# Mamba in a macaron block: the residual is added by TensorE and copied by ScalarE, the normalisation's shift is made by GpSimd

## What is computed

```
x = x + 0.5 * moe(layernorm(x))
x = x + mamba(layernorm(x), weights 1) + mamba(flip(layernorm(x)), weights 2)
x = x + 0.5 * moe(layernorm(x))

mamba: xi, z = split(x @ in_w.T)
       xc    = silu(causal_conv4(xi) + conv_b)              # 256 inner channels
       dt, B, C = split(xc @ xp_w.T)                        # 8, 16, 16
       delta = softplus(dt @ dtp_w.T + dtp_b)
       h_t   = h_{t-1} * exp(delta_t * A) + delta_t * xc_t * B_t      # 16 states
       y     = (sum over states of h_t * C_t + xc * D) * silu(z)
       return y @ out_w.T
```

## Time and profile before

| | |
|---|---|
| Time, median of 3 runs | 2934.28 us (2933.41 to 2934.28) |
| Profiled execution | 2933.32 us, of which its span is 2931.5 us |
| Busy over the span | PE 84%, DVE 85%, POOL 78%, ACT 54%, PEld 52% |
| Mamba's units in the span | about 559 to 2392 us |
| Mean granted PE clock | 0.95 of full speed |

### The profile page before, as it was taken

The page is one execution under the profiler, slowest core; times in us unless marked ns, Lnnn a source line. Parts: engine busy times, 40 slices in busy tenths (PEclk is TensorE's granted clock), DMA queues, the critical chain, the costliest instruction groups (busy, mean ns, idle before and its releaser), DMA issues.

```text
span 2931.5 us, 37910 instructions
## 1 busy us (share of the span) xinstructions
PE 2458.6 (84%) x10844; PEld 1533.2 (52%) x10844; DVE 2495.6 (85%) x3793; ACT 1575.0 (54%) x2744; POOL 2297.3 (78%) x1360
## 2 busy tenths in 40 slices
PE   4799999688888888888888888888888875899993
PEld 2799998233343443344344334433433335899993
DVE  6766666499999999999999999999999988666666
ACT  3355555566556565655656565565656541555551
POOL 1577777489889988889899898889888853777772
PEclk8899999899999999999999999999999988999997
DMA  6011112223333333233233333222322340111116
GB/s 222 14 49 49 49 49 47 72 96 96 105 97 94 96 104 99 94 99 106 87 102 105 92 95 106 97 94 95 102 93 90 99 149 1 45 48 50 49 49 190
DMA packets 159360, 254.71 MB, mean 87 GB/s; under 512 B 22114, under 2 KB 64002, under 8 KB 158594
## 3 DMA queue, kind: packets, MB, share of 16 engines
q1 hardware_dynamic: 140338, 209.21, 22.8%
q0 software_dynamic: 18464, 37.79, 4.8%
q10 hardware_dynamic: 432, 6.29, 0.5%
HBM read 219.65 MB, written 33.55 MB: 86 GB/s over the span
## 4 chain that ended last, share of the span: by engine, by line
DVE 29%; issue 21%; PE 15%; POOL 11%; ACT 5%; DMA 1%; POOLq 0%; DVEq 0%; SPq 0%
DVE buf L830 11%; PE bank L1333 7%; DVE buf L821 6%; DVE bank L806 6%; POOL buf L396 5%; ACT over L1072 3%; POOL buf L454 3%; POOL token_outputs L406 2%; PE bank L1329 2%; PE bank L1275 2%; PE bank L1283 2%; ACT L1043 1%; PE bank L1189 1%; DVE buf L794 1%; DVE X L717 1%
## 5 line engine op out<-in xcount | busy, mean ns | idle before, releaser
L454 POOL TENSOR_TENSOR buf<-buf 128x1024 f32<-128x1024 f32 x512 | 1202.6, 2360 | 197.8 <-DVE buf L830 164.2
L1333 PE MATMUL bank<-buf,id_sb 128*128 128x512 f32 x2048 | 1017.0, 626 | 133.3 <-POOL buf L454 130.5
L830 DVE TENSOR_TENSOR_SCAN buf<-over,bank 128x512 f32<-128x512 f32 x768 | 892.3, 1203 | 1.0
L1072 ACT ACTIVATE over<-wgu,negA 128x510 f32<-128x510 f32 x768 | 505.8, 712 | 555.0 <-DVE buf L830 483.0
L1333 PEld LDWEIGHTS bank<-buf,id_sb 128*128 128x128 f32 x2048 | 395.1, 198 | 568.1 <-issue 350.9
L806 DVE TENSOR_TENSOR bank<-wgu,bank 128x512 f32<-128x512 f32 x768 | 487.2, 681 | 2.5 <-POOL wgu L486 2.5
L1208 PE MATMUL bank<-parts 128*128 128x256 f32 x3456 | 486.4, 291 | 3.2 <-DVE buf L680 1.6
L1208 PEld LDWEIGHTS bank<-parts 128*128 128x128 f32 x3456 | 434.2, 192 | 7.1 <-issue 4.0
L406 POOL DMA_INDIRECT token_outputs<-buf,slot_out x288 | 293.1, 1018 | 110.7 <-issue 85.3
L396 POOL DMA_INDIRECT buf<-token_rows,slot_token x288 | 301.1, 1046 | 96.7 <-issue 90.1
L821 DVE TENSOR_TENSOR_SCAN buf<-bank,buf 128x256 f32<-128x256 f32 x512 | 309.0, 665 | 44.4 <-ACT bank L1081 43.9
(11 more groups left out here) (155 smaller groups left out, 2308.8 us busy)
## 6 DMA issues: line engine op xcount, KB each, us to landing
buf<-state_rows SPq DMA_DIRECT2D x640, 256.0 KB, 3.2
token_rows<-buf SPq DMA_DIRECT2D x32, 256.0 KB, 2.3
y_pair<-token_outputs SPq DMA_DIRECT2D x16, 512.0 KB, 5.1
buf<-token_outputs SPq DMA_DIRECT2D x16, 512.0 KB, 5.0
buf<-token_rows,slot_token POOLq DMA_INDIRECT x288, 2.6
token_outputs<-buf,slot_out POOLq DMA_INDIRECT x288, 2.3
out<-X SPq DMA_DIRECT2D x16, 256.0 KB, 3.9
wgu<-wgT ACTq DMA_DIRECT2D x1, 2048.0 KB, 8.4
```

Source lines behind the costliest of these rows:

```text
L454: pool.tensor_tensor(hC[:, b, :].rearrange("p (c w) -> p c w", c=C), hs[:, b, :].rearrange("p (c w) -> p c w", c=C), Cs[:, b, :].unsqueeze ...
L830: V.tensor_tensor_scan(hs[:, b, w], dA[:, b, c, :, :].rearrange("p s t -> p (s t)"), bank[c], 0.0, ALU.mult, ALU.add).then_inc(s[f"scan_do ...
L1072: ins = A.activation(dA[:, n % R, c, :, 1:], delta[r][:, c * W:(c + 1) * W].rearrange("p (s t) -> p s t", s=S)[:, :, 1:], ACT.Exp, scale=n ...
L1333: ins = M.matmul(bank[4 + c], id_sb[:, :], hC[:, n % R, c * W:(c + 1) * W], start=False, stop=(n == NS - 1), skip_group_check=True)
```

## The change

Three things are changed.

- `project_out` on PE gets, for each of the four tiles, one more matmul that adds X to bank 7 through the identity. It has one more wait, for the residual of the unit before (it reads the X which that one wrote).
- `post_residual` on DVE is removed. ACT copies bank 7 to X instead (`residual`) at the same state, 8, and for the last unit ahead of the second mixture-of-experts part.
- `mean_shift` on DVE is removed. POOL's `rstd` makes -mean ahead of var + eps, and -mean times rstd behind the power, both 128x4. `normalise` waits for that.

```diff
-DVE_AT = {"gate": 2, "stats": 5, "lo": 8, "res": 8, "shift": 9, "size": 12}
+DVE_AT = {"gate": 2, "stats": 5, "lo": 8, "size": 12}
-ACT_AT = {"silus": 4, "hi": 7, "parts": 10, "ln": 11, "xn": 12, "scale": 13, "xnT": 15}
+ACT_AT = {"silus": 4, "hi": 7, "res": 8, "parts": 10, "ln": 11, "xn": 12, "scale": 13, "xnT": 15}
...
             def rstd(p):
                 pool.wait_ge(s["dve_norm"], done(DVE_NORM, "aggr", p))
                 pool.sem_inc(s["rstd_turn"], 1)
+                pool.tensor_scalar(ve[:, G:2 * G], MV[:, :, 0], -1.0, None, ALU.mult)
                 pool.tensor_scalar(ve[:, 0:G], MV[:, :, 1], EPS, None, ALU.add).then_inc(s["vareps_pre"], 1)
                 pool.wait_ge(s["vareps_pre"], p + 1)
                 pool.tensor_tensor(rs[:, 0:G], ve[:, 0:G], half[:, 0:G], ALU.pow).then_inc(s["rstd_pre"], 1)
+                pool.wait_ge(s["rstd_pre"], p + 1)
+                pool.tensor_tensor(shift[:, :], ve[:, G:2 * G], rs[:, 0:G], ALU.mult).then_inc(s["shift_pre"], 1)
...
-            def mean_shift(p):
-                dve.wait_ge(s["rstd_pre"], p + 1)
-                dve.wait_ge(s["dve_norm"], done(DVE_NORM, "aggr", p))
-                V.scalar_tensor_tensor(out=shift[:, :], in0=MV[:, :, 0], scalar=-1.0, in1=rs[:, 0:G],
-                                       op0=ALU.mult, op1=ALU.mult).then_inc(s["dve_norm"], 1)
...
-            def post_residual(u, p, r):
-                dve.wait_ge(s["pe_post"], u + 1)
-                xp4 = X[:, bass.ds(p * G, G), :]
-                V.tensor_tensor(xp4, xp4, bank[7].rearrange("p (t d) -> p t d", t=G),
-                                ALU.add).then_inc(s["res_done"], 1)
...
-                act.wait_ge(s["dve_norm"], done(DVE_NORM, "shift", p))
+                act.wait_ge(s["shift_pre"], p + 1)
...
+            def residual(u, p):
+                act.wait_ge(s["pe_post"], u + 1)
+                A.activation(X[:, p * G:(p + 1) * G, :], bank[7].rearrange("p (t d) -> p t d", t=G),
+                             ACT.Copy).then_inc(s["res_done"], 1)
...
+                        if n == ACT_AT["res"] and not (first and r == 0):
+                            residual(p * 2 + r - 1, p - 1 if r == 0 else p)
...
             pair(NP - 1, False, True)
+            residual(2 * NP - 1, NP - 1)
             act.wait_ge(s["res_done"], 2 * NP)
...
             def project_out(u, r, after):
                 pe.wait_ge(s["gated"], u + 1)
+                wait(pe, s["res_done"], u)
                 after()
                 for t in range(G):
                     for c in range(C):
-                        ins = M.matmul(bank[7][:, t * D:(t + 1) * D], gat[:, c * W + t * P:c * W + (t + 1) * P],
-                                       out_sb[:, r, c, :], start=(c == 0), stop=(c == C - 1))
+                        M.matmul(bank[7][:, t * D:(t + 1) * D], gat[:, c * W + t * P:c * W + (t + 1) * P],
+                                 out_sb[:, r, c, :], start=(c == 0), stop=False)
+                    ins = M.matmul(bank[7][:, t * D:(t + 1) * D], id_sb[:, :], X[:, (u // 2) * G + t, :],
+                                   start=False, stop=True)
                 ins.then_inc(s["pe_post"], 1)
```

More of the change, by code:

```diff
@@ L38 @@
     "conv0_", "conv1_", "z0_", "z1_", "xdbl", "dt0_", "dt1_")]
-DVE_NORM = ["stats", "aggr", "shift"]
+DVE_NORM = ["stats", "aggr"]
 ACT_NORM = ["xn", "xnT", "xnTrev"]
-DVE_AT = {"gate": 2, "stats": 5, "lo": 8, "res": 8, "shift": 9, "size": 12}
+DVE_AT = {"gate": 2, "stats": 5, "lo": 8, "size": 12}
 POOL_AT = {"first": 0, "second": 1, "rstd": 7, "du": 13}
-ACT_AT = {"silus": 4, "hi": 7, "parts": 10, "ln": 11, "xn": 12, "scale": 13, "xnT": 15}
+ACT_AT = {"silus": 4, "hi": 7, "res": 8, "parts": 10, "ln": 11, "xn": 12, "scale": 13, "xnT": 15}
 PE_AT = {"conv": 0, "z": 5, "xdbl": 6, "out": 7, "dt": 9, "xt": 13}
@@ L260, in macaron_kernel @@
             experts_done expA_done pair_added dtp_zeroed diag_ready taps_spread taps_ready skip_ready gated du_done dve_pre
-            act_pre pe_pre vareps_pre rstd_pre res_done pe_post negA_done bcB_ready bc_copied bc_stored C_in0 C_in1 C_in2 C_in3 B_in0 B_in1 dA_ready
+            act_pre pe_pre vareps_pre rstd_pre shift_pre res_done pe_post negA_done bcB_ready bc_copied bc_stored C_in0 C_in1 C_in2 C_in3 B_in0 B_in1 dA_ready
             dP_ready0 dP_ready1 mul_done pool_mul_done scan_done0 scan_done1 hC_ready y_done""".split()
@@ L569, in moe @@
                     if m == 1 and j == 0:
-                        post_residual(2 * NP - 1, NP - 1, 1)
                         dve.wait_ge(s["res_done"], 2 * NP)
@@ L846, in pair @@
                             product(p, r, n + 1)
-                        if not (first and r == 0):
-                            if n == DVE_AT["res"]:
-                                post_residual(u - 1, p - 1 if r == 0 else p, 1 - r)
                         if not prep:
@@ L858, in pair @@
                                 layernorm(p + 1)
-                            if n == DVE_AT["shift"]:
-                                mean_shift(p + 1)
             layernorm(0)
-            mean_shift(0)
             split_lo(0, 0)
```

## The result

| | before | after |
|---|---|---|
| Time, median | 2934.28 us (4 runs, 2933.41 to 2936.96) | 2893.24 us (4 runs, 2890.67 to 2893.94) |
| Ratio to before | | 0.9855, 95% interval 0.9843 to 0.9866 |
| Profiled execution (its span) | 2933.32 us (2931.5) | 2893.94 us (2892.1) |

The change makes the kernel 41.0 us faster, 39.4 us by the profiled executions; 44.1 was predicted, and 2890 us for the time. In the kernel after, the lines are L784 for the gate, L820 for the scan, L811 for the scan of POOL's four states, L796 for the product, L772 for `split_lo`, L457 for `times_C`, L444 for POOL's product, L1070 for the decay into a bank, L1061 for the other decays and L1051 for the residual's copy.

The account below looks back on a forecast made before the run. DVE, 97% busy in the Mamba part, was taken to bound it from state 8's scan to the next gate, PE and ACT before that. 22.7 + 21.8 - 0.4 = 44.1 us off 2933.32 gave 2889.2, median 2890, range 2885 to 2896.

Parts of the forecast that it names:

- The loop of two parts: Mamba unit: PE and ACT set the time from gate to state 8's scan, DVE from there to the next gate.
- Residual: DVE at state 8: removing the addition saves 0.71 us in each of 31 units, 22.0 us.
- Shift: DVE at state 9: removal saves 21.8 us over 15, nearly all of it waiting for POOL's instruction to end.
- Shift on POOL: POOL at state 7 of 15 units: the new work takes 0.6 us (0.3 to 2.0) and costs nothing in the units.
- The far end of 2.0 us: Highest price of POOL's new work at state 7; state 11's product would still come 0.2 us before its scan.
- the cover at state 11: POOL's product for state 11, with 0.6 us of new work ahead, still has 1.6 us to spare before DVE's scan.
- X through PE, residual on ACT: State 7 matmuls, 1.0 us, and ACT's copy, 0.58 us, cost nothing; without cover 31 and 18.6 us.
- First pair and last residual: First pair's shift on POOL costs 0.4 us; the 32nd residual, in the second mixture-of-experts part, saves 0.7 us.
- The clock rival: PE's chain behind the gate at 1.2 GHz: 12.7 us more a unit, 2954 us with five; chance 0.04.

Follow-up runs that it names:

- e8: Kernel after plus an unused 128x512 DVE reduction at state 6 of every unit: 2896.19 us, ratio to before 0.9862.
- e9: Kernel after plus an unused 128x512 DVE reduction at state 10 of every unit: 2914.91 us, ratio to before 0.9924.
- e2: Kernel before with only the shift moved from DVE to POOL: 2912.81 us against 2937.24 before, ratio 0.9919.
- e6: Kernel after plus an unused 128x4 DVE operation with two SBUF inputs at state 9 of first directions: 2902.12 us, ratio to before 0.9881.
- e7: Kernel after plus an unused 128x4 DVE maximum with one SBUF input at state 9 of first directions: 2902.22 us, ratio to before 0.9883.
- e1: Kernel after with the shift back on DVE at state 9, so only the residual's half: 3079.31 us on a slower chip, ratio to before 0.9957.
- e11: Kernel after plus two unused 128x4 powers on POOL ahead of the shift's multiplication: 2915.62 us, ratio to before 0.9922.
- e3: Kernel before with PE's four extra matmuls, DVE copying bank 7 instead of adding it: 3093.55 us against 3093.14 before, ratio 1.000.
- e4: Kernel after with a second ACT copy of bank 7, ahead of the residual's: ratio to before 0.9875.
- e5: Kernel after with PE's whole output projection made twice into the same bank: ratio to before 0.9849.

## Why the prediction was right, and where a size was off

*The loop of two parts.* Right. The idle time ahead of the scan of state 8 stayed at 0.71 and 1.99 us, both removed steps lay behind it, and e8 and e9 show the same work free ahead of it and full price behind it.

*Residual.* This is the mis-sized term. The start-to-start 0.71 us of the removed instruction was taken as what its removal gives. It isn't, because the instruction behind it then meets another neighbour: `split_lo` can't overlap the product as the residual could. Measured is 0.60 (1.89 to 1.29): 31 x 0.60 = 18.6 instead of 22.0 us, 3.4 less (18.3, 3.7 less, by the gates). It is the largest mechanism in the 3.2 us between 2890 and 2893.24; the books below have the rest.

*Shift.* Right. A pair of units went from 113.93 to 111.18, so 2.75 us less, of which 1.18 are two residuals (0.59 each by the gates) and 1.57 the shift. Fourteen shifts lay between the first gate and the last: 22.0 us, as e2 has it by itself; 21.8 was predicted for fifteen. The fifteenth is in the first unit, where it met the end of POOL's instruction (0.20 us, which the mean of 1.53 holds), and gave nothing: the way to the first gate was 64.52 and is 64.54 us from the first product. e6 and e7 confirm the reason. What the prediction left out is that this wait also takes back gains ahead of it: by e1 the residual alone gives 10.1 us between the gates, 12 but for its late units, and not the 22.0 of its term. Because both parts were made together, the sum of the two terms holds; for the residual alone the same working would have promised nearly double.

*Shift on POOL.* Right: 0.23 and 0.20 us, 0.55 with their issue (0.6 predicted), and no DVE idle time for POOL. The far end of 2.0 us was costed at nothing, and no run tests it. e11's wait bears out the cover at state 11 (2.2 us), but its 2.7 us cost 20 in all, twice what first directions explain, by late units that the working does not have.

*X through PE, residual on ACT.* Right, both hidden: e3, e4 and e5. The projection is 2.84 us, 2.9 predicted; 1.95 before, so 0.9 more and not 1.0.

*First pair and last residual.* The shift of the first pair came 0.39 us later, 0.4 predicted. The last unit's residual gave its 0.7 us up to the step behind it (from the last gate to the shift of the experts' part 12.06 us before, 11.35 after), but behind the last gate only 0.2 us of it were left.

*The books.* Of the profiled difference of 39.4 us, 40.74 lie between the first gate and the last: 18.3 residual (0.59 a unit by the gates), 22.0 shift, 0.4 from units longer than the regular ones. The end gives 0.2, the way from the layer normalisation to the first product 0.5 (PE's convolution there took 8.73 instead of 9.63 us), and the first layer normalisation began 2.05 us later, in the mixture-of-experts part, which no edit touches. The 0.5 and 0.4 gained and the 2.05 lost are nothing that the prediction worked out; that they come to no more than 1.2 us is luck.

*The clock rival.* It did not decide, but its mechanism is there. One first direction of the kernel after took 56.99 us. Rows of that unit, first the clock ahead of its gate, then DVE's gate, PE's first work for it and the scan of state 8:

```profile
1671.00:1681.00 10.00, 9.42 (x17) 3.91 (x16) 10.00 (x13) 2.90 (x5) 10.00 (x6) 0.67 0.35 106
1674.20:1677.60 3.40, 3.40 (x6) 1.34 (x5) 3.40 (x5) 1.33 (x2) 3.40 (x3) 0.51 0.54 145
...
1681.60 1.26 DVE L784 TENSOR_TENSOR buf<-bank,wgu 128x512 f32<-128x512 f32 x2
...
1684.42 1.88 PE L1324 MATMUL bank<-wgu,skip_sb 128*128 128x512 f32 x4
...
1702.27 1.85 DVE L811 TENSOR_TENSOR_SCAN buf<-bank,buf 128x256 f32<-128x256 f32 x3 [2.12 <-ACT bank L1070]
```

The gate ends at 1682.86 and PE begins 1.56 us later, since its queue was behind after a stretch at 0.67, with 3.4 us at 0.51 in it, the 1.2 GHz level. Such a late unit costs mostly 1.3 to 1.5 us, about what the earlier trace rows said (0.9 and 1.8 at the extremes), and but for e11 a profiled execution had one to four of them. All traces agree: in the 28 late units the lower level ended 3.4 to 4.2 us ahead of the gate and PE began 1.5 to 1.6 us behind the gate's end; in the other 375 it ended over 7 us ahead or wasn't there, and PE began within 0.06 us. The prediction looked for low clock behind the gate; it comes ahead of it.

## What to carry to other kernels

Find the loop and the wait in it before costing an edit: the same operation of some 0.67 us on the fullest engine was free at state 6 and cost 0.59 us a turn at state 10. Price a removal from the start of the instruction ahead to the start of the one behind, and ask whether these two neighbours can overlap. A tiny operation whose duration ends with another engine's instruction is a wait for that instruction: it absorbs what is saved ahead of it, so remove it together with the savings.

## What the hardware showed that was not expected

- A 128x4 operation on DVE with two inputs in SBUF took 0.16, 0.59, 1.65 and 2.25 us, in each of the last three ending within 0.02 us of the end of POOL's instruction; started 0.06 us ahead of it, 0.15. With one input it took 0.15, however POOL's instructions lay.
- An operation over more partitions and elements (104x512 against 40x512) was cheaper by 0.18 us, starting at the same partition as its neighbours.
- On PE an fp32 matmul of 128x128 shows as two records, and twelve of them took 2.84 us, 0.22 for each matmul from start to start (0.67 for a tile's three).
- POOL's 128x4 negation and multiplication took 0.23 and 0.20 us, a power of the same size 1.04.
